# A two-layer graph network over eight graphs: one wait of VectorE moved, one row of reciprocals made on TensorE, one mean computed from a sum

## The chip, the cores and the metric

The kernel runs on one core of one Trainium2 chip. The metric is the device time of one execution in microseconds (us). The median of three runs of the kernel before is 1084.4 us, and the runs lie between 1082.91 and 1084.53 us. Engines are called TensorE (PE in the profile; PEld is its weight load), VectorE (DVE), ScalarE (ACT), GpSimd (POOL) and SyncE (SP).

## The reference, cut to what matters

There are eight graphs, each with 1024 nodes, node features `x` [1024, 256] and a dense-stored adjacency `adj` [1024, 1024] with many zeros. `W1` is [512, 256], `W2` is [256, 512] and `W` is [256, 512].

```
H   = (adj != 0);  w = adj[0, :]
D   = 1 / (H @ w)            per node,  0 where the sum is not positive
Be  = 1 / H.sum(axis=0)      per hyperedge
conv(v, W, b) = D * (H @ (Be * (H.T @ (v @ W.T)))) + b
h   = layer_norm(relu(conv(x, W1, b1)), gamma, beta)
x1  = norm(x + conv(h, W2, b2) + x)
deg = adj.sum(axis=1);  agg = (adj @ x1) / max(deg, 1e-6)
out = norm(x1 + relu(concat(x1, agg) @ W.T))
```

## The kernel before, in words

All eight graphs are worked on one core, one after the other. Nodes are cut into eight tiles of 128 and the 1024 columns into two chunks of 512. Products that need more precision than one pass gives are split into a high and a low part (`x_hi`, `x_lo` and so on).

One graph goes through these stages on TensorE, in this order. S1 forms `H.T @ x` (for graph 0 this happens in the setup, for a later graph at the end of the graph before it). S2 forms `H` times that, transposed, in four jobs: two for the first chunk of nodes (banks 2 and 3) and two for the second (banks 4 and 5). P and M, job by job (eight of each, `j`), apply `W1` to `z`, the S2 result scaled by 1/degree. Q multiplies the hidden layer `hT` by `W2` (eight jobs `i`; the first five, `Q_FIRST`, stand ahead of S3, the other three between the steps of S3). Each Q job ends with a one-column product from the sums of squares `ssum`. S3 and S4 are the second convolution, V, VM and L the second layer, and then comes S1 of the next graph. The order of the instructions on each engine is written out by hand, and semaphores join the engines.

Between S2 and P stands a chain on three engines: VectorE multiplies the S2 result by `w_row` (`scale_z`, L876), ScalarE rounds it (L609, L611), VectorE forms the low part (`take_z_low`, L882), and only then P may start. `w_row` must hold the row of 1/degree on all 128 partitions. VectorE makes 1/degree as a column, `rDn` [128, 8] (`build_rDn`, L742 to L747), and ScalarE's queue stores it to DRAM and loads it back as a row on all partitions (L602 and L599). For graphs 1 to 7 this is done in the V and L stages of the graph before. For graph 0 it is done in the setup, after VectorE's last degree sum (`sum_Dn`, L735).

In P, VectorE squares each chunk of the hidden layer (L899) and GpSimd adds the squares up (L461, semaphore `squares_summed`, six sums a graph). In Q, VectorE's `take_q(i)` (L904, L751, L911) normalises the Q job and frees its bank. Job 4 uses the bank of job 0. Two of the next graph's degree sums, for tiles 0 and 1, stand behind `take_q(5)` and `take_q(6)` (`DN_IN_Q`). They write a throwaway result into `unread_Q`, which lies on the third slot of `hpre`, the buffer that GpSimd's last sum reads. The kernel has one wait for this ahead of the first `take_q`:

```
if more:
    dve.wait_ge(squares_summed, b * NSQ + NSQ)
for i in range(NT):
    take_q(i)
    next_Dn(DN_IN_Q.get(i, ()), unread_Q)
```

`more` is false for graph 7, so that graph has no such wait.

In the setup, TensorE also forms the column mean of the scaled second weight: four f32 products of 256 columns, `mean_n` against `gW2T[:, k]`, added in one bank (L1111), in the middle of the S1 job of tile 6. ScalarE copies it out as `W2_mean` (L584) behind the first of its copies `take_m_hi` (L539), and GpSimd subtracts it from the four blocks of the weight (L426). VectorE's order there is: the split of `W1` (L824, L829), the hyperedge reciprocals (L817, L820), `take_m_lo` (L767) in turn with the last two blocks of `HT` (L774), and then the degree sums of tiles 3 to 7. After `rDn` is ready GpSimd adds `b2` to the residual in eight operations (L439).

Of the kernel before, what the change touches and what calls it, by code (L numbers as in the profile page):

```python
# [5 lines left out]
F32 = mybir.dt.float32  # L6
F32R = mybir.dt.float32r
BF16 = mybir.dt.bfloat16
ALU = mybir.AluOpType
ACT = mybir.ActivationFunctionType  # L10

P = 128
# [22 lines left out]
TRANSPOSE_BANKS = (6, 7)  # L35
N_BANKS = 8
Q_FIRST = 5
T_SLOTS = 3
FIRST_DN_AT = (4, 6)
X1_SLOTS = 3  # L40
# [2 lines left out]
DN_IN_Q = {5: (0,), 6: (1,)}  # L43
# [3 lines left out]
def graph_net(nc, x, adj, W1, b1, gamma, beta, W2, b2, WL, out):  # L47
    B, C, D = x.shape
    DH = W1.shape[0]
    NT = C // P  # L50
    ND = D // P
    NH = DH // P
    CH = 512
    NCH = C // CH
# [10 lines left out]
    NSQ = NCH * (NH - 1)  # L65
# [6 lines left out]
    N_SIDE = TRANSPOSE_BANKS[0]  # L72
# [55 lines left out]
    with ctx:  # L128
# [3 lines left out]
        def place(name, shape, dt, offset=None):  # L132
            n = 4 if dt != BF16 else 2
            for d in shape[1:]:
                n *= d
            if offset is None:
                offset = at[0]
                at[0] += (n + 63) // 64 * 64
            return nc.alloc_sbuf_tensor_at(name, shape, dt, offset=offset), offset, offset + (n + 63) // 64 * 64

        raw, raw_at, _ = place("raw", [P, NT, C], F32)
        H, H_at, _ = place("H", [P, NT, C], F32R)
# [32 lines left out]

        adjB, _, _ = place("adjB", [P, NT, NB, RB], F32, raw_at)

        yv, _, nxt = place("yv", [P, NT, YP], F32, HT_at)
        o_f32, _, nxt = place("o_f32", [P, 2, D], F32, nxt)
        unread_Q, _, _ = place("unread_Q", [P, C], BF16, hpre_at + 4 * CH * (T_SLOTS - 1))  # L180
# [17 lines left out]
        gamma_n, _, nxt = place("gamma_n", [P, P], F32, nxt)  # L198
        mean_n, _, nxt = place("mean_n", [P, P], F32, nxt)
        assert nxt <= m_lo_at + 4 * NT * D and m_lo_at == m_hi_at + 4 * NT * D  # L200
        W2_mean = ssum_0[:, 0:D]
        W1T, _, _ = place("W1T", [P, ND, DH], F32, xres_at)

        def col(n):
# [13 lines left out]
        def sem(name):  # L218
            return ctx.enter_context(nc.semaphore(name))
# [11 lines left out]
                              "gamma_loaded", "beta_loaded", "bias_loaded",  # L231
                              "table_loaded"))
        row_stored, row_loaded = sem("row_stored"), sem("row_loaded")
        rDn_dram = nc.dram_tensor("rDn_row", [C], F32)
        ident_zero, ident_ready, zero_ready, eps_ready, ones_ready, x_split, x_hi_done, xb_part, xb_ready = (
            sem(n) for n in ("ident_zero", "ident_ready", "zero_ready", "eps_ready", "ones_ready", "x_split", "x_hi_done",
# [4 lines left out]
        be_done, rBe_ready, m_hi_done = (sem(n) for n in ("be_done", "rBe_ready", "m_hi_done"))  # L241
        relu_done, squared, squares_summed, msq_done = (
            sem(n) for n in ("relu_done", "squared", "squares_summed", "msq_done"))
        mean_ready, unit_ready, W2_mean_done, W2_centred = (
            sem(n) for n in ("mean_ready", "unit_ready", "W2_mean_done", "W2_centred"))
        z_high_done, z_high_scaled, z_low_done, z_cross_done = (
            sem(n) for n in ("z_high_done", "z_high_scaled", "z_low_done", "z_cross_done"))
        W1_high_done, W1_low_done, W1_cross_done = (
# [25 lines left out]
        def emptied(stage, tile, b):  # L274

            n = bank_of[stage, tile]
            return bank_empty[n], b * fills[n] + (setup_empties[n] + nth[stage, tile] + 1)
# [10 lines left out]
        def set_empty(name, part):  # L288
            tb, turn = set_of[name, part]
            return bank_empty[tb], turn + 1  # L290
# [10 lines left out]
        def over_graphs(eng, graph):  # L301


            with eng.Fori(0, B - 1) as b:
                graph(b, True)
            graph(B - 1, False)
# [98 lines left out]
        def _(pool):  # L405
# [11 lines left out]
            def split_x(b):  # L417

                pool.wait_ge(x_hi_done, b)
                for t in range(NT):  # L420
                    nc.gpsimd.tensor_tensor(x_lo[:, t, :], x_in[:, t, :], x_hi[:, t, 0:D].bitcast(F32), ALU.subtract)\
                      .then_inc(x_split, 1)

            pool.wait_ge(W2_mean_done, 1)
            for k in range(NH):
                nc.gpsimd.tensor_tensor(gW2T[:, k, 0:D], gW2T[:, k, 0:D], W2_mean, ALU.subtract).then_inc(W2_centred, 1)  # L426
# [76 lines left out]
        def _(act):  # L503
# [75 lines left out]
                          .then_inc(W1_high_done, 1)  # L579
            for e in range(NT):  # L580
                take_m_hi("S1", e, 0, e)
                if e == 0:
                    act.wait_ge(*set_full("bW2", 0))
                    nc.scalar.activation(W2_mean, set_bank("bW2", 0)[:, D:2 * D], ACT.Copy).then_inc(W2_mean_done, 1)  # L584
                    nc.scalar.activation(bW2_row[:, :], set_bank("bW2", 0)[:, 0:D], ACT.Copy)\  # L585
                      .then_inc(bank_empty[set_of["bW2", 0][0]], 1)
# [8 lines left out]
                act.dma_start(rDn_dram.rearrange("(t p) -> p t", p=P), rDn, allow_slow_non_contiguous=True).then_inc(row_stored, 16)  # L595

            def load_rDn_row(b):
                act.wait_ge(row_stored, b * 16 + 16)
                act.dma_start(w_row[:, :], rDn_dram[:].partition_broadcast(P)).then_inc(row_loaded, 16)  # L599

            act.wait_ge(rDn_ready, 1)
            act.dma_start(rDn_dram.rearrange("(t p) -> p t", p=P), rDn, allow_slow_non_contiguous=True).then_inc(row_stored, 16)  # L602
            load_rDn_row(0)

            def graph(b, more):
                def take_z_high(ch, d):
# [110 lines left out]
        def _(dve):  # L717
# [21 lines left out]
            def build_rDn(b):  # L739

                dve.wait_ge(dn_ready, b * NT + NT)
                nc.vector.tensor_scalar(dn_pos, dn, 0.0, None, ALU.is_gt).then_inc(rDn_part, 1)  # L742
                nc.vector.tensor_scalar(dn_safe, dn, TINY, None, ALU.max).then_inc(rDn_part, 1)
                dve.wait_ge(rDn_part, b * 3 + 2)
                nc.vector.reciprocal(dn_inv, dn_safe).then_inc(rDn_part, 1)
                dve.wait_ge(rDn_part, b * 3 + 3)
                nc.vector.tensor_tensor(rDn, dn_inv, dn_pos, ALU.mult).then_inc(rDn_ready, 1)  # L747
# [117 lines left out]
            for t in range(4 + NT - N_SIDE, NT):  # L865
                sum_Dn(t, 0, unread, (first_rows_loaded[t], 16))
            build_rDn(0)

            def graph(b, more):
                dve.wait_ge(rDn_ready, b + 1)  # L870
# [58 lines left out]
                def next_Dn(tiles, into):  # L929
                    if more:  # L930
                        for c in tiles:
                            sum_Dn(c, b + 1, into, (raw_loaded[c // 2], (b + 1) * IN_B))

                if more:
                    dve.wait_ge(squares_summed, b * NSQ + NSQ)
                for i in range(NT):
                    take_q(i)
                    next_Dn(DN_IN_Q.get(i, ()), unread_Q)
                if more:
                    dve.wait_ge(q_split, b * NT + NT)  # L940
                next_Dn((2, 3), unread)
# [86 lines left out]
        def _(pe):  # L1028
# [55 lines left out]
            def transpose_set(name, part):  # L1084
                if name == "W1":
                    pe.wait_ge(W1_loaded, 16)
                    transpose_four("W1", part, [W1n[:, h, part * P:(part + 1) * P] for h in range(NH)])
                elif name == "WL":
                    pe.wait_ge(WL_loaded, 16)
                    transpose_four("WL", part, [WLn[:, o, (side * ND + part) * P:(side * ND + part + 1) * P]  # L1090
                                                for side in range(2) for o in range(ND)])
                elif name == "W2":
                    pe.wait_ge(W2_loaded, 16)
                    transpose_four("W2", part, [W2n[:, o, k * P:(k + 1) * P]
                                                for k in (2 * part, 2 * part + 1) for o in range(ND)])
                elif name == "gamma":
                    pe.wait_ge(gamma_loaded, 32)
                    tb, turn = set_of["gamma", 0]
                    pe.wait_ge(bank_empty[tb], turn)
                    nc.tensor.transpose(banks[tb][:, 0:2 * NH], gamma_n[0:2 * NH, :], ident[0:2 * NH, 0:2 * NH])\  # L1100
                      .then_inc(bank_full[tb], 1)
                else:
                    pe.wait_ge(bW2_wide_done, ND)
                    pe.wait_ge(mean_ready, 1)
                    for part in range(NH // 2):
                        pe.wait_ge(*set_empty("W2", part))
                    pe.wait_ge(W2T_scaled, NH // 2)
                    tb, turn = set_of["bW2", 0]
                    pe.wait_ge(bank_empty[tb], turn)
                    for k in range(NH):  # L1110
                        mm(banks[tb][:, D:2 * D], mean_n[:, :], gW2T[:, k, 0:D], start=(k == 0), stop=(k == NH - 1))  # L1111
                    for o in range(ND):
                        last = nc.tensor.transpose(banks[tb][:, o * P:(o + 1) * P], bW2_wide[:, o, :], ident[:, :])
                    last.then_inc(bank_full[tb], 1)
# [19 lines left out]
            for e in range(N_SIDE, NT):  # L1134
                pe.wait_ge(*free("S1", e, 0))
                for c in range(NT):
                    if e == N_SIDE and c == NT - 3:
                        transpose_set("bW2", 0)
                    s1_step(e, c, 0)
            def graph(b, more):  # L1140
                def s2_step(ch, k):

                    for d in range(ND):
                        job = ch * ND + d
                        if k == 0:
                            pe.wait_ge(*free("S2", job, b))
                        for n, m in enumerate((m_hi, m_lo)):
                            last = mm(bank("S2", job)[:, :], m[:, k, d * P:(d + 1) * P],  # L1148
                                      HT[:, k, ch * CH:(ch + 1) * CH], start=(k == 0 and n == 0),
                                      stop=(k == NT - 1 and n == 1))  # L1150
                        if k == NT - 1:
                            fills_bank(last, "S2", job)
# [8 lines left out]

                for k in range(NT):
                    s2_step(1, k)

                for j in range(NJ):
                    ch, f = j // NH, j % NH
# [86 lines left out]
                                pe.wait_ge(H_ready, (b + 1) * NT + c + 1)  # L1253
                            s1_step(e, c, b + 1)

            over_graphs(pe, graph)


# [22 lines left out]
```

## Time and profile before

| | |
|---|---|
| Median of three runs | 1084.4 us (1082.91 to 1084.53) |
| The profiled execution, its own time | 1085.47 us |
| Its span, first to last instruction | 1083.7 us |
| TensorE busy | 1045.8 us, 97% of the span |
| VectorE busy | 772.2 us, 71% |
| ScalarE busy | 432.4 us, 40% |
| GpSimd busy | 427.4 us, 39% |
| Mean granted TensorE clock | 0.990 |

The own time of the profiled execution is 1.77 us more than its span. TensorE is busy nearly all the time, so what counts is when it isn't, and at what granted clock it runs. [...] An f32 product is recorded as two instructions, so four of them are "x8".

### The profile page before, as it was taken

To read this page: it belongs to the slowest core of one execution; us is meant where nothing else is said; L and a number is where in the kernel's file an instruction comes from. 1 tells how busy PE (TensorE), PEld (TensorE's weight loads), DVE (VectorE), ACT (ScalarE), POOL (GpSimd) and SP (SyncE) were. 2 spreads that over 40 slices of the span, in tenths; PEclk is the share of its full clock that TensorE was granted. 3 is DMA by queue.
4 is the path that set the end of the run, shared out by engine and by line. 5 is a ranking of instruction groups with operands and counts; after the bars stand their busy time and mean duration, and the time that the engine had idled before them with its cause. 6 is when DMAs were issued, how large, how long until landed. Compare 5 with 4: busy or idle time off the path is not lost.

```text
span 1083.7 us, 19718 instructions
## 1 busy us (share of the span) xinstructions
PE 1045.8 (97%) x6243; PEld 939.4 (87%) x6243; DVE 772.2 (71%) x1846; ACT 432.4 (40%) x1027; POOL 427.4 (39%) x671
## 2 busy tenths in 40 slices
PE   8859999999999999999999999999999999999997
PEld 8749989798887989889898898988989889898986
DVE  6566786768857778577886687866787767867355
ACT  5353622436125362243523444243532536225350
POOL 0333535434254341553425443343535425255320
PEclk9979999999999999999999999999999999999999
DMA  7036440533407144072432634126341444400001
GB/s 286 1 98 137 98 98 20 131 82 97 106 10 174 39 99 105 17 167 74 102 76 49 146 99 100 32 69 144 97 92 24 114 99 97 97 20 1 1 2 39
DMA packets 73211, 90.44 MB, mean 83 GB/s; under 512 B 16601, under 2 KB 62305, under 8 KB 73185
## 3 DMA queue, kind: packets, MB, share of 16 engines
q1 hardware_dynamic: 63232, 85.49, 33.8%
q10 hardware_dynamic: 9952, 4.63, 1.8%
q8 instruction: 13, 0.21, 0.1%
q14 instruction: 14, 0.11, 0.0%
HBM read 81.66 MB, written 8.42 MB: 83 GB/s over the span
## 4 chain that ended last, share of the span: by engine, by line
PE 66%; issue 15%; POOL 12%; DVE 6%; ACT 1%; DMA 0%; POOLq 0%; DVEq 0%; ACTq 0%
PE bank L1047 43%; PE bank L1194 6%; POOL xres L439 4%; POOL z_cross L454 3%; POOL ssum L461 3%; PE bank L1237 3%; PE bank L1230 3%; PE bank L1231 3%; PE bank L1077 3%; DVE hpre L899 2%; PE bank L1148 1%; PE bank L1211 1%; POOL xres L433 1%; PE bank L1038 1%; ACT hpre L620 1%
## 5 line engine op out<-in xcount | busy, mean ns | idle before, releaser
L1047 PE MATMUL bank<-yv,adjT 128*128 128x257 f32 x1024 | 223.3, 379 | 0.0
L1047 PEld LDWEIGHTS bank<-yv,adjT 128*128 128x128 f32 x1024 | 193.8, 189 | 28.4
L544 ACT ACTIVATE small<-mv,small 128x1 f32<-128x1 f32 x192 | 55.9, 291 | 265.6 <-DVE mv L762 146.8
L1194 PE MATMUL bank<-gW2T,hT 128*128 128x257 f32 x512 | 125.4, 388 | 12.9 <-DVE q_f L911 12.9
L1047 PE MATMUL bank<-x_hi,H 128*128 128x256 f32 x512 | 126.4, 288 | 0.0
L1077 PE MATMUL bank<-x_hi,H 128*128 128x258 f32 x512 | 124.6, 290 | 0.0
L1047 PE MATMUL bank<-x_lo,H 128*128 128x256 f32 x512 | 123.5, 282 | 0.0
L1047 PE MATMUL bank<-m_hi,HT 128*128 128x256 f32 x512 | 122.0, 281 | 0.0
L1047 PE MATMUL bank<-m_lo,HT 128*128 128x256 f32 x512 | 121.4, 280 | 0.0
L1077 PE MATMUL bank<-x_lo,H 128*128 128x256 f32 x512 | 120.1, 283 | 0.0
L1194 PEld LDWEIGHTS bank<-gW2T,hT 128*128 128x128 f32 x512 | 93.8, 191 | 25.0 <-DVE q_f L911 13.5
L539 ACT ACTIVATE m_hi<-bank,small 128x256 fp32r<-128x256 f32 x128 | 57.5, 474 | 137.0 <-DVE small L812 76.9
L1148 PE MATMUL bank<-HT,m_lo 128*128 128x512 f32 x256 | 101.9, 398 | 0.0
L1148 PE MATMUL bank<-HT,m_hi 128*128 128x512 f32 x256 | 100.8, 394 | 0.1
L1047 PEld LDWEIGHTS bank<-x_hi,H 128*128 128x128 f32 x512 | 98.0, 191 | 0.0
L1047 PEld LDWEIGHTS bank<-x_lo,H 128*128 128x128 f32 x512 | 97.6, 191 | 0.0
L445 POOL TENSOR_TENSOR small<-mv,small 128x1 f32<-128x1 f32 x120 | 30.1, 251 | 169.6 <-DVE small L751 169.6
L767 DVE SCALAR_TENSOR_TENSOR m_lo<-bank,small,m_hi 128x256 fp32r<-128x256 f32 x128 | 59.4, 482 | 52.6 <-ACT m_hi L539 52.6
L1047 PEld LDWEIGHTS bank<-m_lo,HT 128*128 128x128 f32 x512 | 96.2, 188 | 0.0
L1047 PEld LDWEIGHTS bank<-m_hi,HT 128*128 128x128 f32 x512 | 96.1, 188 | 0.0
L1077 PEld LDWEIGHTS bank<-x_hi,H 128*128 128x128 f32 x512 | 94.2, 191 | 0.5 <-ACT bW_row L585 0.2
L1077 PEld LDWEIGHTS bank<-x_lo,H 128*128 128x128 f32 x512 | 93.5, 190 | 0.2
(125 smaller groups left out, 2191.7 us busy)
## 6 DMA issues: line engine op xcount, KB each, us to landing
raw<-in_adj_dram SPq DMA_DIRECT2D x112, 256.0 KB, 5.7
adjB<-in_adj_dram SPq DMA_DIRECT2D x224, 128.0 KB, 3.1
x_in<-in_x_dram SPq DMA_DIRECT2D x31, 256.0 KB, 6.3
out_dram<-xres SPq DMA_DIRECT2D x108, 64.0 KB, 1.6
raw<-in_adj_dram SPq DMA_DIRECT2D x8, 512.0 KB, 8.9
w_row<-in_adj_dram SPq DMA_DIRECT2D x8, 512.0 KB, 4.7
w_row<-rDn_row ACTq DMA_DIRECT2D x8, 512.0 KB, 9.2
out_dram<-xres SPq DMA_DIRECT2D x4, 256.0 KB, 2.6
```

The costliest lines, as they stand in the source:

```text
L439: nc.gpsimd.tensor_tensor(xres[:, t, :], xres[:, t, :], b2_row[:, :], ALU.add).then_inc(xb_ready, 1)
L454: nc.gpsimd.tensor_tensor(z_cross[:, d, cols], z_high[:, d, cols].bitcast(F32), z_low[:, d, cols].bitcast(F32), ALU.subtract).then_inc(z_c ...
L461: nc.gpsimd.tensor_tensor(ssum[j // NH][:, :], ssum[j // NH][:, :], hpre[:, j % T_SLOTS, :], ALU.add)\
L539: nc.scalar.activation(m_hi[:, e, :], bank(stage, e)[:, 0:D], ACT.Identity, scale=rBe[:, e:e + 1])\
L544: nc.scalar.activation(std[:, i:i + 1], mv[:, which, i, 1:2], ACT.Sqrt, bias=eps_c)\
L767: empties_bank(nc.vector.scalar_tensor_tensor(out=m_lo[:, e, :], in0=bank(stage, e)[:, 0:D], scalar=rBe[:, e:e + 1], in1=m_hi[:, e, :].bit ...
L1047: last = mm(bank(stage, i)[:, 0:n_cols], lhsT, rhs, start=(k == 0 and part == 0), stop=(k == NT - 1 and part == parts - 1))
L1077: last = mm(*args, start=(c == 0 and n == 0), stop=(c == NT - 1 and n == 1))
L1148: last = mm(bank("S2", job)[:, :], m[:, k, d * P:(d + 1) * P], HT[:, k, ch * CH:(ch + 1) * CH], start=(k == 0 and n == 0), stop=(k == NT - ...
L1194: mm(bank("Q", i)[:, 0:D + 1], hT[:, k, i * P:(i + 1) * P], gW2T[:, k, :], start=(k == 0), stop=(k == NH - 1))
L1230: mm(bank("V", i)[:, :], x1_high[n][:, part], WL_high[:, d, :], start=(d == 0), stop=False)
L1231: last = mm(bank("V", i)[:, :], x1_low[:, n, part], WL_low[:, d, :], start=False, stop=(d == ND - 1))
```

## The change

VectorE's wait for `squares_summed` goes from ahead of the first `take_q` to just ahead of each of the two degree sums in `DN_IN_Q`. For graph 0, VectorE fills a 128x128 tile of ones and multiplies the identity by `rDn`, both broadcast, into eight diagonal blocks; TensorE multiplies the ones by the diagonals, two f32 products of 512 columns into banks 0 and 1, behind the third step of S2's second chunk; ScalarE copies the two banks to `w_row`. The store and the load through DRAM remain for graphs 1 to 7. For this TensorE's program has graph 0 written out ahead of its loop, which then runs over graphs 1 to 6. For the mean, GpSimd adds the four blocks of the weight in three dependent operations, TensorE makes one product of the sum, and ScalarE takes the result behind its sixth copy `take_m_hi` and not behind the first.

```diff
+        diagonals, _, nxt = place("diagonals", [P, NT, P], F32, raw_at)
+        ones, _, _ = place("ones", [P, P], F32, nxt)
...
+            pool.wait_ge(W2T_scaled, NH // 2)
+            for part in range(NH // 2):
+                pool.wait_ge(*set_empty("W2", part))
+            for k in range(1, NH):
+                if k > 1:
+                    pool.wait_ge(W2_summed, k - 1)
+                nc.gpsimd.tensor_tensor(W2_sum, gW2T[:, 0, 0:D] if k == 1 else W2_sum, gW2T[:, k, 0:D], ALU.add)\
+                  .then_inc(W2_summed, 1)
             pool.wait_ge(W2_mean_done, 1)
...
                 take_m_hi("S1", e, 0, e)
-                if e == 0:
+                if e == N_SIDE - 1:
                     act.wait_ge(*set_full("bW2", 0))
...
-                act.wait_ge(row_stored, b * 16 + 16)
+                act.wait_ge(row_stored, b * 16)
...
-            act.wait_ge(rDn_ready, 1)
-            act.dma_start(rDn_dram.rearrange("(t p) -> p t", p=P), rDn, allow_slow_non_contiguous=True).then_inc(row_stored, 16)
-            load_rDn_row(0)
+            for ch in range(NCH):
+                act.wait_ge(row_full, ch + 1)
+                nc.scalar.activation(w_row[:, ch * CH:(ch + 1) * CH], banks[ROW_BANKS[ch]][:, :], ACT.Copy)\
+                  .then_inc(row_loaded, 16 // NCH)
...
             build_rDn(0)
+            nc.vector.memset(ones[:, :], 1.0).then_inc(ones_set, 1)
+            dve.wait_ge(rDn_ready, 1)
+            dve.wait_ge(ident_ready, 1)
+            nc.vector.tensor_tensor(diagonals[:, :, :], ident[:, :].unsqueeze(1).to_broadcast([P, NT, P]),
+                                    rDn.unsqueeze(2).to_broadcast([P, NT, P]), ALU.mult).then_inc(diagonals_done, 1)
...
-                if more:
-                    dve.wait_ge(squares_summed, b * NSQ + NSQ)
                 for i in range(NT):
                     take_q(i)
-                    next_Dn(DN_IN_Q.get(i, ()), unread_Q)
+                    if more and i in DN_IN_Q:
+                        dve.wait_ge(squares_summed, b * NSQ + NSQ)
+                        next_Dn(DN_IN_Q[i], unread_Q)
...
-                    for part in range(NH // 2):
-                        pe.wait_ge(*set_empty("W2", part))
-                    pe.wait_ge(W2T_scaled, NH // 2)
+                    pe.wait_ge(W2_summed, NH - 1)
                     tb, turn = set_of["bW2", 0]
                     pe.wait_ge(bank_empty[tb], turn)
-                    for k in range(NH):
-                        mm(banks[tb][:, D:2 * D], mean_n[:, :], gW2T[:, k, 0:D], start=(k == 0), stop=(k == NH - 1))
+                    mm(banks[tb][:, D:2 * D], mean_n[:, :], W2_sum, start=True, stop=True)
...
+            def make_row():
+                pe.wait_ge(ones_set, 1)
+                pe.wait_ge(diagonals_done, 1)
+                for ch in range(NCH):
+                    pe.wait_ge(*emptied("S1", ROW_BANKS[ch], 0))
+                    mm(banks[ROW_BANKS[ch]][:, :], ones[:, :], diagonals[:, ch * 4:ch * 4 + 4, :],
+                       start=True, stop=True).then_inc(row_full, 1)
...
                 for k in range(NT):
                     s2_step(1, k)
+                    if first and k == ROW_BEHIND:
+                        make_row()
...
-            over_graphs(pe, graph)
+            graph(0, True, True)
+            with pe.Fori(1, B - 1) as b:
+                graph(b, True)
+            graph(B - 1, False)
```

## Rows read from the trace of the kernel before

**Rows 1.** The page's busy time of each engine, with share and instructions.

```profile
PE 1045.8 (97%) x6243; PEld 939.4 (87%) x6243; DVE 772.2 (71%) x1846; ACT 432.4 (40%) x1027; POOL 427.4 (39%) x671
```

**Rows 2.** TensorE's waits: who for whom, us in total, times, longest.

```profile
PE bank L1174 <- DVE z_low L882: 13.9, 1, 13.9
PE bank L1194 <- DVE q_f L911: 12.9, 7, 2.0
```

**Rows 3.** Timeline of graph 1's Q: start, us, instruction, idle and releaser.

```profile
206.73 1.91 PE L1194 MATMUL bank<-gW2T,hT 128*128 128x257 f32 x8
...
215.33 0.22 DVE L904 SCALAR_TENSOR_TENSOR mv<-bank,mv 128x1 f32<-128x1 f32 x1 [2.50 <-POOL ssum L461]
...
216.64 2.01 PE L1194 MATMUL bank<-gW2T,hT 128*128 128x257 f32 x8 [2.00 <-DVE q_f L911]
```

**Rows 4.** The same timeline for graph 7, which lacks the wait.

```profile
990.96 1.91 PE L1194 MATMUL bank<-gW2T,hT 128*128 128x257 f32 x8
...
996.94 0.21 DVE L904 SCALAR_TENSOR_TENSOR mv<-bank,mv 128x1 f32<-128x1 f32 x1
...
998.73 1.99 PE L1194 MATMUL bank<-gW2T,hT 128*128 128x257 f32 x8
...
999.52 1.33 POOL L465 TENSOR_TENSOR x_lo<-q_f,x_hi 128x256 fp32r<-128x256 f32 x2
```

**Rows 5.** Windows of graph 2 behind its wait; PEclk stands behind POOL.

```profile
346.80:350.00 3.20, 3.19 (x12) 2.77 (x13) 1.63 (x7) 1.81 (x9) 1.39 (x3) 0.69 1.02 210
350.00:353.30 3.30, 3.30 (x19) 3.08 (x18) 1.42 (x5) 0.75 (x4) 1.36 (x2) 0.78 0.74 153
```

**Rows 6.** Timeline: the row's way in graph 0, and graph 1's first P job.

```profile
44.97 0.40 ACTq L602 DMA_DIRECT2D rDn_row<-small  x1
45.07 5.57 POOL L439 TENSOR_TENSOR xres<-xres,b_row 128x256 f32<-128x256 f32 x8 [8.58 <-DVE small L747]
...
60.51 1.29 DVE L876 TENSOR_TENSOR z_f<-bank,w_row 128x512 f32<-128x512 f32 x2 [15.57 <-DMA w_row<-rDn_row]
...
65.05 0.80 PE L1174 MATMUL bank<-z_high,W_high 128*128 128x512 f32 x1 [13.93 <-DVE z_low L882]
65.07 1.29 POOL L454 TENSOR_TENSOR z_cross<-z_high,z_low 128x512 fp32r<-128x512 f32 x1 [0.62 <-DVE z_low L882]
...
195.53 0.39 PE L1174 MATMUL bank<-z_high,W_high 128*128 128x512 f32 x1
```

**Rows 7.** TensorE's timeline: the first and the last of graph 0's 64 S2 products.

```profile
35.94 0.47 PE L1148 MATMUL bank<-HT,m_hi 128*128 128x512 f32 x1
...
50.71 0.40 PE L1148 MATMUL bank<-HT,m_lo 128*128 128x512 f32 x1
```

**Rows 8.** TensorE's timeline of graph 0: Q's job 0 and job 4.

```profile
77.73 1.90 PE L1194 MATMUL bank<-gW2T,hT 128*128 128x257 f32 x8
...
86.48 2.01 PE L1194 MATMUL bank<-gW2T,hT 128*128 128x257 f32 x8 [0.84 <-DVE q_f L911]
```

**Rows 9.** Timeline of the setup: the mean, its copy, its user, VectorE behind it.

```profile
30.81 1.89 PE L1111 MATMUL bank<-gW2T,mean_n 128*128 128x256 f32 x8
...
32.96 0.38 ACT L584 ACTIVATE ssum<-bank 128x256 f32<-128x256 f32 x1 [2.02 <-PE bank L1113]
...
33.42 3.07 POOL L426 TENSOR_TENSOR gW2T<-gW2T,ssum 128x256 f32<-128x256 f32 x4 [31.83 <-ACT ssum L584]
...
34.01 0.48 DVE L767 SCALAR_TENSOR_TENSOR m_lo<-bank,small,m_hi 128x256 fp32r<-128x256 f32 x1 [1.95 <-ACT m_hi L539]
```

**Rows 10.** Timeline: one VectorE operation beside GpSimd's work and without it.

```profile
140.61 5.35 POOL L421 TENSOR_TENSOR x_lo<-x_in,x_hi 128x256 fp32r<-128x256 f32 x8 [3.99 <-DVE H L724]
...
142.17 0.72 DVE L1008 SCALAR_TENSOR_TENSOR xres<-o_f,xres 128x256 f32<-128x256 f32 x1
...
149.11 0.42 DVE L1008 SCALAR_TENSOR_TENSOR xres<-o_f,xres 128x256 f32<-128x256 f32 x1
```

**Rows 11.** VectorE's operations of 1024 elements with two SBUF inputs: count, busy, mean ns.

```profile
L735 DVE SCALAR_TENSOR_TENSOR unread<-raw,w_row 128x1024 bf16<-128x1024 f32 x50 | 61.0, 1220 | 9.5 <-POOL x_lo L465 9.1
```

More of the change, by code:

```diff
@@ L37 @@
 Q_FIRST = 5
+ROW_BANKS = (0, 1)
+ROW_BEHIND = 2
 T_SLOTS = 3
@@ L200, in graph_net @@
         assert nxt <= m_lo_at + 4 * NT * D and m_lo_at == m_hi_at + 4 * NT * D
-        W2_mean = ssum_0[:, 0:D]
+        W2_mean, W2_sum = ssum_0[:, 0:D], ssum_0[:, D:2 * D]
         W1T, _, _ = place("W1T", [P, ND, DH], F32, xres_at)
@@ L233, in graph_net @@
         row_stored, row_loaded = sem("row_stored"), sem("row_loaded")
+        ones_set, diagonals_done, row_full = sem("ones_set"), sem("diagonals_done"), sem("row_full")
         rDn_dram = nc.dram_tensor("rDn_row", [C], F32)
@@ L243, in graph_net @@
             sem(n) for n in ("relu_done", "squared", "squares_summed", "msq_done"))
-        mean_ready, unit_ready, W2_mean_done, W2_centred = (
-            sem(n) for n in ("mean_ready", "unit_ready", "W2_mean_done", "W2_centred"))
+        mean_ready, unit_ready, W2_summed, W2_mean_done, W2_centred = (
+            sem(n) for n in ("mean_ready", "unit_ready", "W2_summed", "W2_mean_done", "W2_centred"))
         z_high_done, z_high_scaled, z_low_done, z_cross_done = (
@@ L1139, in _, with graph @@
                     s1_step(e, c, 0)
-            def graph(b, more):
+            def make_row():
[5 more added lines that the diff above has]
+                       start=True, stop=True).then_inc(row_full, 1)
+            def graph(b, more, first=False):
                 def s2_step(ch, k):
```

## The prediction

> **What bounds the kernel now.** I read the busy times first: TensorE is busy for 97% of the span, so no other engine's share can matter except where TensorE waits for it [rows 1]. Next I read TensorE's own waits. Two entries hold 26.8 us: once 13.9 us before the first P product, and seven times, 12.9 us in all and 2.0 us at most, in Q [rows 2]. The change works on just these two places. Then I followed each in the timeline.
>
> In Q of graph 1, VectorE stands idle for 2.50 us until GpSimd's last sum is there, starts `take_q(0)` at 215.33, and TensorE, which needs the bank of job 0 for job 4, starts again at 216.64 after 2.00 us [rows 3]. Graph 7 has no such wait in its program: there `take_q(0)` has no idle time before it and job 4 follows at once [rows 4]. It is a built-in view of the kernel without the wait. [...]
>
> In graph 0, VectorE has `rDn` ready by 45.07 (GpSimd's release), but the row is on all partitions only at 60.51, after 15.57 us of idle time on VectorE, and P starts at 65.05 [rows 6]. TensorE's last S2 product began at 50.71 [rows 7].
>
> **The wait in Q.** Nothing is removed but order: the same sums and the same degree sums are done. From the start of job 0 to that of job 4 graph 1 takes 216.64 - 206.73 = 9.91 us [rows 3] and graph 7 takes 998.73 - 990.96 = 7.77 us [rows 4]. The difference is 2.14 us. Graphs 1 to 6 all wait 2.00 us, graph 0 waits 0.84 us and takes 86.48 - 77.73 = 8.75 us, 0.98 over graph 7 [rows 8]. That is 6 x 2.14 + 0.98 = 13.8 us. The fallen clock costs 3.20 x 0.31 + 3.30 x 0.22 = 1.7 us in graph 2 [rows 5] and as much in graph 6, 3.4 us together. I count it as gained, since it begins where TensorE's idle time ends. Sum: 17.2 us.
>
> What is late next? VectorE is free at 215.33 - 2.50 = 212.83, and `take_q(0)` frees the bank 216.64 - 215.33 = 1.31 us after it starts, so at 214.14, 7.41 us after job 0 began [rows 3]. TensorE gets to job 4 at 7.77 us. There is 0.36 us to spare, little, but on the right side. The one-column product of job 4 waits for the same sums, yet only behind job 4's four products, and S3 needs GpSimd's first `x_lo`, which in graph 7 starts 8.56 us after job 0 without any idle time on TensorE [rows 4]. The wait now stands ahead of the degree sums of tiles 0 and 1; behind it are `take_q(6)`, `take_q(7)` and VectorE's S3 work. It costs nothing, because `take_q(5)` needs Q's job 5, which is filled after job 4 and so after all sums. SP's loads are tied to the ends of P and Q, so they move with TensorE. Bounds: 13.8 us if the two falls of the clock come back elsewhere, 17.2 us if not.
>
> **The mean.** Four products of 256 columns take 1.89 us; one takes a quarter, so TensorE's S2 starts 1.4 us earlier, near 34.5 instead of 35.94 [rows 7, 9]. GpSimd's three dependent additions cost it some 2.4 us (3.07 / 4 = 0.77 each for independent ones [rows 9]). GpSimd is idle for 31.83 us before its first use [rows 9], and the second half of the weight is copied well before 30.81, so TensorE should not wait. ScalarE no longer stands in front of the bank of the mean with four `m_hi` copies behind it, so VectorE's 1.95 us of idle time at 34.01 goes [rows 9]. On the other side, GpSimd's additions run beside the splitting of `W1` and its subtractions (3.07 us) move beside the degree sum of tile 3. A VectorE operation with two SBUF inputs took 0.72 us beside GpSimd and 0.42 us alone, 1.7 times as long [rows 10]. I put back 1.15 us for this. Then `rDn` is ready 0.8 us earlier, at 44.3. Bounds: 43.1 (the whole 1.95 gained) and 45.07 (nothing).
>
> **The row.** It has these steps. (a) The fill with ones is an operation of 128 columns, about 0.1 us. (b) The diagonals have 1024 elements and two SBUF inputs. The nearest row is the degree sum, 1.22 us [rows 11]. But GpSimd's eight additions, 5.57 us, are released by the same `rDn` [rows 6], so I take 1.22 x 1.7 = 2.1 us. With one semaphore the diagonals are there at 44.3 + 2.3 = 46.6. Bounds: 1.22 and 2 x 1.22 us, so 44.5 to 47.7. (c) TensorE passes the third step of the second chunk, 44 of 64 products at (50.71 - 35.94) / 63 = 0.234 us each [rows 7], at 34.5 + 10.3 = 44.8. It waits for 1.8 us, until R = 46.6; R lies between 44.8 and 47.7. (d) Two f32 products of 512 columns have the columns of the four of 256, 1.89 us [rows 9]; this is new work on TensorE. (e) ScalarE's copy of 256 columns takes 0.38 us [rows 9], one of 512 perhaps 0.6. The row stands at R + 1.9 + 0.1 + 0.6 = R + 2.6. (f) From there to P it took 65.05 - 60.51 = 4.54 us [rows 6], so P starts at R + 7.1. TensorE has the row and the remaining 20 products behind it at R + 1.9 + 4.7 = R + 6.6, and waits another 0.5 us. (g) P's first M job needs GpSimd's second `z_cross`, which started with P and took 1.29 us [rows 6], while four P products at 0.234 take 0.94: 0.4 us more. In effect P starts at R + 7.5 = 54.1.
>
> Before, P started at 65.05, and P and its neighbour to Q took 77.73 - 65.05 = 12.68 us [rows 6, 8] against 206.73 - 195.53 = 11.20 in graph 1 [rows 3, 6]; 1.48 us went to the clock that had fallen in the long wait. So the old effective start is 66.5 and the gain 66.5 - 54.1 = 12.4 us. Bounds: R = 44.8 gives 14.2, R = 47.7 gives 11.3.
>
> [...]
>
> **TensorE's loop.** Graph 0 is now a copy of its own. Graph 7 is also run from a copy of its own, and its P stage to Q is entered as in graph 1: its job 0 to 4 of Q show no gap [rows 4]. I cost this at nothing; above it I have no row.
>
> **The sum.** 17.2 + 12.4 = 29.6 us off the profiled execution's 1085.47: 1055.9 us. That execution is 1.07 us above the median of 1084.4, less than one fall of the clock costs (1.7 us). I read this as one fall more in it than in a middling run, and since the new kernel should have none, I start from the profiled one. From the median the same step would be 28.5 us.
>
> **The rivals.**
>
> 1. *The clock falls in other places.* Graph 0 keeps short waits of 1.8, 0.5 and 0.4 us. Waits of 2.0 us brought the clock down in two cases of six. One fall costs 1.7 us, two cost 3.4: 1057.6 to 1059.3. For it: the first of these waits is nearly as long. Against it: five waits in Q did nothing. Chance 0.15.
>
> 2. *GpSimd blocks the diagonals wholly.* They then run behind the eight additions: 44.3 + 5.6 + 1.3 = 51.2 = R. P starts in effect at 58.7, a gain of 7.8 us, less 1.7 us for a clock that falls in a wait of 6.4 us. The total is 23.3 us: 1062.2. Against it stands 1.7 times, not more, beside eight additions in a row [rows 10]. Chance 0.08.
>
> 3. *The wait in Q is replaced.* The spare time is only 0.36 us, and VectorE's steps now run beside GpSimd's last sums. If TensorE still waits for 1 us in each of seven graphs, Q gives 10.2 us and the total is 22.6: 1062.9. If it is the whole 2.0 us (the change doesn't do what it says), 12.4 us remain: 1073.1. Against both stands graph 7. Chance 0.07.
>
> 4. *Slower.* Entering the loop at graph 1 for the first time could make TensorE wait for code that it had met before in graph 0. It decides if this one place costs over 29.6 us; with 35 us the time is 1090.9. Nothing in the trace shows such a gap at the entry of graph 7's copy. Chance 0.02.
>
> **How the numbers follow.** The forecast has the remaining 0.68; its own range is 1054.1 (R = 44.8) to 1057.0 (R = 47.7), and half a microsecond either way for differences of executions. With the first rival this holds 0.83, and the range is 1053.6 to 1059.6. The bound of what a measurement can tell is 0.2%, 2.2 us. All cases but the fourth are faster by more: 0.97. Same: 0.01. Slower: 0.02.
>
> **What would show it.** Right: no TensorE wait for `q_f` in graphs 0 to 6, 7.8 us from job 0 to job 4, and a clock of 1.00 behind it; the diagonals done near 46.6 in over 2 us beside GpSimd; P's first product near 53.7; the mean's product under 0.5 us. Wrong: a wait of job 4 or S3 in its place; the diagonals taking over 4 us; an S2 that waits for the last `m_lo`, which VectorE now must have ready 1.4 us sooner; low granted clock in graph 0 behind the row.

## The result and the profile after

The changed kernel takes 1055.93 us (median of four runs, 1055.58 to 1056.11), the kernel before 1083.87 us (median of four runs, one more than was known before; 1082.91 to 1084.53). The ratio is 0.9742 with a 95% interval of 0.9726 to 0.9759: 27.9 us, 2.6% faster. The profiled execution of the changed kernel also takes 1055.93 us and has a span of 1054.1 us. The forecast was 1055.9 us, so the total was met; but that it was met so closely is luck: inside it, two steps were wrong and cancelled each other.

The page of the changed kernel, busy time of each engine, against [rows 1]:

```profile
PE 1040.4 (99%) x6241; PEld 934.0 (89%) x6241; DVE 774.5 (73%) x1848; ACT 433.5 (41%) x1029; POOL 430.1 (41%) x674
```

TensorE's waits in the changed kernel, against [rows 2]:

```profile
PE bank L1059 <- DMA raw<-in_adj_dram: 4.5, 1, 4.5
PE bank L1098 <- ACT bW_row L600: 1.6, 1, 1.6
PE bank L1202 <- DVE z_low L903: 1.0, 1, 1.0
PE bank L1059 <- ACT adjT L564: 0.6, 1, 0.6
PE bank L1210 <- POOL z_cross L469: 0.2, 1, 0.2
```

The 13.9 us ahead of P have become 1.0 and the 12.9 us in Q are gone from the list. A new row stands there: TensorE waits 1.6 us for ScalarE's copy of the mean's bank (L600). The forecast had no such row.

Graph 1's Q in the changed kernel, timeline of all engines, against [rows 3]:

```profile
193.42 1.90 PE L1222 MATMUL bank<-gW2T,hT 128*128 128x257 f32 x8
...
199.08 2.91 POOL L476 TENSOR_TENSOR ssum<-ssum,hpre 128x512 f32<-128x512 f32 x2 [0.71 <-DVE hpre L920]
...
199.44 0.21 DVE L925 SCALAR_TENSOR_TENSOR mv<-bank,mv 128x1 f32<-128x1 f32 x1
...
200.21 0.48 DVE L932 SCALAR_TENSOR_TENSOR q_f<-bank,small,bW_row 128x256 f32<-128x256 f32 x1
...
201.19 1.99 PE L1222 MATMUL bank<-gW2T,hT 128*128 128x257 f32 x8
...
201.94 1.34 POOL L480 TENSOR_TENSOR x_lo<-q_f,x_hi 128x256 fp32r<-128x256 f32 x2
```

VectorE now starts `take_q(0)` at 199.44, beside GpSimd's last sums, and is through with it at 200.69. TensorE starts job 4 at 201.19, 7.77 us after job 0, exactly as graph 7 did before [rows 4]. The bank is free 0.5 us before it is needed. The granted clock in this place, a share of full speed, in windows of graphs 1, 2 and 6 (PEclk behind POOL), against [rows 5]:

```profile
193.00:201.00 8.00, 8.00 (x41) 7.00 (x40) 6.95 (x12) 4.83 (x11) 4.39 (x4) 1.00 0.77 177
321.00:329.00 8.00, 8.00 (x41) 6.99 (x40) 6.98 (x12) 4.79 (x11) 4.38 (x5) 1.00 0.82 187
833.00:841.00 8.00, 8.00 (x41) 6.99 (x40) 7.00 (x12) 4.77 (x11) 4.38 (x5) 1.00 0.82 179
```

From Q to Q every graph now takes 128.0 us. Before, it was 129.0 us from graph 0 to 1, 130.2 us behind each later graph, and 131.8 us where the clock fell. From Q's job 0 of graph 0 to that of graph 7 it is 896.1 us; before, it was 913.2. These 17.1 us are what the moved wait gave between the two profiled executions.

The setup of graph 0, timeline, against [rows 6, 9]:

```profile
30.70 0.59 PE L1129 MATMUL bank<-ssum,mean_n 128*128 128x256 f32 x2
...
32.41 0.48 DVE L783 SCALAR_TENSOR_TENSOR m_lo<-bank,small,m_hi 128x256 fp32r<-128x256 f32 x1
...
33.32 0.43 ACT L600 ACTIVATE bW_row<-bank 128x256 f32<-128x256 f32 x1
...
33.55 4.71 POOL L441 TENSOR_TENSOR gW2T<-gW2T,ssum 128x256 f32<-128x256 f32 x4 [4.26 <-ACT ssum L599]
...
33.80 0.39 PE L1098 MATMUL bank<-x_hi,H 128*128 128x258 f32 x1 [1.58 <-ACT bW_row L600]
...
35.81 0.40 PE L1174 MATMUL bank<-HT,m_hi 128*128 128x512 f32 x1
...
43.23 1.20 DVE L887 TENSOR_TENSOR diagonals<-ident,small 128x1024 f32<-128x1024 f32 x1
...
43.31 6.55 POOL L454 TENSOR_TENSOR xres<-xres,b_row 128x256 f32<-128x256 f32 x8 [5.05 <-DVE small L763]
...
46.08 1.88 PE L1163 MATMUL bank<-diagonals,ones 128*128 128x512 f32 x4
...
48.39 0.60 ACT L618 ACTIVATE w_row<-bank 128x512 f32<-128x512 f32 x1 [0.59 <-PE bank L1163]
...
49.02 1.29 DVE L897 TENSOR_TENSOR z_f<-bank,w_row 128x512 f32<-128x512 f32 x2 [4.59 <-ACT w_row L618]
...
51.98 1.55 DVE L903 SCALAR_TENSOR_TENSOR z_low<-z_f,z_cross 128x512 fp32r<-128x512 f32 x1 [0.35 <-ACT z_cross L627]
...
53.67 0.47 PE L1202 MATMUL bank<-z_high,W_high 128*128 128x512 f32 x1 [1.04 <-DVE z_low L903]
...
65.38 1.90 PE L1222 MATMUL bank<-gW2T,hT 128*128 128x257 f32 x8
```

The mean is one product, recorded as two instructions (x2), of 0.59 us, but S2 starts at 35.81, hardly before the old 35.94 [rows 7]. The diagonals take 1.20 us and are done at 44.43, and TensorE comes to the row's products 1.65 us later, at 46.08, without waiting for anything. P starts at 53.67 in place of 65.05 [rows 6], and Q's job 0 at 65.38 in place of 77.73 [rows 8].

### The profile page after: what moved, and what is told of

The parts are those of the page before. It is cut to its first block, busy times and chain, and to the rows that moved or that the text cites. A ratio compares the mean times of both kernels' runs of the same rounds, so it can differ in the third digit from the quotient of the medians.

```text
span 1054.1 us, 19674 instructions
## 1 busy us (share of the span) xinstructions
PE 1040.4 (99%) x6241; PEld 934.0 (89%) x6241; DVE 774.5 (73%) x1848; ACT 433.5 (41%) x1029; POOL 430.1 (41%) x674
## 4 chain that ended last, share of the span: by engine, by line
PE 96%; DVE 1%; POOL 1%; issue 1%; DMA 0%; ACT 0%; POOLq 0%; DVEq 0%; ACTq 0%
PE bank L1068 44%; PE bank L1098 11%; PE bank L1222 11%; PE bank L1174 10%; PE bank L1210 3%; PE bank L1258 3%; PE bank L1265 3%; PE bank L1203 3%; PE bank L1259 3%; PE bank L1202 3%; PE bank L1239 1%; PE bank L1059 1%; PE bank L1225 1%; DVE unread L751 1%; POOL xres L454 0%
## 5 line engine op out<-in xcount | busy, mean ns | idle before, releaser
L1222 PEld LDWEIGHTS bank<-gW2T,hT 128*128 128x128 f32 x512 | 93.0, 190 | 11.5
## 6 DMA issues: line engine op xcount, KB each, us to landing
adjB<-in_adj_dram SPq DMA_DIRECT2D x224, 128.0 KB, 3.3
```

The source lines that it names most:

```text
L1222: mm(bank("Q", i)[:, 0:D + 1], hT[:, k, i * P:(i + 1) * P], gW2T[:, k, :], start=(k == 0), stop=(k == NH - 1))
```

## The experiments

The kernel before was run again beside each group; its median was 1083.01 us beside the first four, 1083.93 beside the next four and 1084.09 beside the last two.

**The moved wait alone, on the kernel before.**

```diff
-                if more:
-                    dve.wait_ge(squares_summed, b * NSQ + NSQ)
                 for i in range(NT):
                     take_q(i)
-                    next_Dn(DN_IN_Q.get(i, ()), unread_Q)
+                    if more and i in DN_IN_Q:
+                        dve.wait_ge(squares_summed, b * NSQ + NSQ)
+                        next_Dn(DN_IN_Q[i], unread_Q)
```

> The kernel before with the moved wait alone. Theory (graph 7 shows what is left): TensorE has no wait for q_f in any graph, 7.8 us from job 0 to job 4 of Q in graphs 1 to 6; 13.8 us less, and up to 3.4 us more where the clock fell in the run compared: 1067 to 1070 us. Rival (only the idle time counts and the clock falls anyway): 12.9 us less and the granted clock still falls below 0.85 in Q of some graph: 1071 us or more.

Measured: 1067.35 us, ratio 0.9861 (0.9845 to 0.9877), 15.7 us less. TensorE has no wait for `q_f` left. From Q to Q the graphs take 128.0 us each, and no fall of the clock is left in Q; from job 0 of graph 0 to that of graph 7 it is 896.1 us, as in the changed kernel. If 13.8 us of the 15.7 are stall, 1.9 us remain, more than one fall of the clock and less than two. The rival falls: the clock did not fall elsewhere.

**The row alone, on the kernel before.** The edit is the row's part of the diff above, with the old wait and the old mean.

> The kernel before with the row of graph 0 made on TensorE alone. rDn stays at 45.1; the diagonals are done at 46.4; the row's products start at 46.4 and P near 54.1. Theory: P's gain is 12.0 us, but graph 0 then waits 2.0 us in Q as the other graphs do and not 0.84, since P no longer runs at a low clock: net 10.8 us less, about 1073 us. Rival (the two parts add up without touching each other): 12 us less and still 0.8 us of wait in graph 0's Q, 1072 us; the profile's wait decides.

Measured: 1071.51 us, ratio 0.9901 (0.9885 to 0.9918), 11.5 us less. TensorE's waits in this kernel:

```profile
PE bank L1217 <- DVE q_f L924: 13.0, 7, 2.0
...
PE bank L1205 <- POOL z_cross L461: 1.2, 1, 1.2
```

Q's job 0 starts at 65.47, 12.26 us sooner than before and within 0.1 us of the whole change's 65.38. That already says what the mean is worth in company. The row's products start at 45.94 and P at 52.75, sooner than the 46.4 and 54.1 that were expected: the single diagonals operation took 1.20 us here too and ended at 45.84. Graph 0's wait in Q is 0.95 us, so neither 2.0 (theory) nor 0.84 unchanged (rival): the first M job waited 1.2 us here, and the engines that sum the squares lag TensorE less for it. That this is the cause is argued, not tested; the expected net gain of 10.8 us was 0.7 too small.

**The mean alone, on the kernel before.**

> The kernel before with the second weight's mean alone. Theory: TensorE saves 1.3 us on the products and loses 1.6 us in front of S1's tile 7, whose bank ScalarE now empties late, so S2 starts at 35.8 to 35.9 as before; but VectorE has rDn 1.8 us sooner (43.3), and since the row's way through DRAM decides P, the time falls by about 1.8 us, to 1082 us. Rival 1 (the products' time counts): S2 starts near 34.5. Rival 2 (no path is touched): no change, P at 65.0.

Measured: 1081.61 us (1080.46 to 1084.96), ratio 0.9994 (0.9985 to 1.0004). The time can't be told from no change. The median is 1.4 us below the 1083.01 of the kernel before beside it, but two of the ten runs took 1084.9 us, at a mean granted clock of 0.988 against 0.991 or 0.992 in the others. The profile can be read in spite of it. Timeline of its setup:

```profile
33.23 0.39 PE L1092 MATMUL bank<-x_hi,H 128*128 128x258 f32 x1 [1.58 <-ACT bW_row L600]
...
42.44 0.17 DVE L762 TENSOR_TENSOR small<-small 128x8 f32<-128x8 f32 x1
...
42.64 0.40 ACTq L617 DMA_DIRECT2D rDn_row<-small  x1
...
53.25 0.36 ACTq L614 DMA_DIRECT2D w_row<-rDn_row  x1
...
57.17 1.29 DVE L891 TENSOR_TENSOR z_f<-bank,w_row 128x512 f32<-128x512 f32 x2 [14.57 <-DMA w_row<-rDn_row]
```

TensorE loses 1.58 us at S1's tile 7, for a bank that ScalarE empties late, and gains 1.3 us on the products: nothing. VectorE has `rDn` sooner: it starts the last operation for it at 42.44, against 44.63 in the kernel with the wait alone, whose setup is the old one. S2 starts at 35.24 here and at 35.80 there, and of these 0.6 us some are inputs that landed sooner in this run, so `rDn` gained about 1.7 us. P starts at 61.72. The row's way through DRAM, though, took 57.17 - 42.64 = 14.5 us here, 60.51 - 44.97 = 15.5 us in the profile before [rows 6] and 59.08 - 44.83 = 14.3 us in the kernel with the wait alone, whose way is the old one; it varies by about as much as the effect. The theory's path is seen, its 1.8 us is not shown in the time.

**The old wait, put back in the changed kernel.**

> The changed kernel with the old wait in Q put back. Theory: seven waits of 2.0 us, graph 0 included, each 2.14 us from job 0 to job 4, so 15.0 us more than the changed kernel, and 0 to 3.4 us for falls of the clock behind them: 1071 to 1074.5 us, with a wider spread than 0.6 us between runs. Rival (graph 0 keeps its 0.84): 13.8 us more.

Measured: 1071.76 us (1071.67 to 1072.18), 15.8 us more than the changed kernel. Graph 0 waits 1.52 us, six graphs 2.0 us each, and the clock fell once. The changed kernel was not run beside this one: the kernel before had a median of 1083.01 us here and 1083.87 there, so some 0.9 us of this difference are open. The two profiles need no such comparison: from Q's job 0 of graph 0 to that of graph 7 it is 912.2 us against 896.1, 16.1 us more. The theory's sum holds; its 2.0 us for graph 0 was too much, the rival's 0.84 too little. The spread of 0.5 us between runs is no wider than that of the changed kernel; a wider one had been expected.

**ScalarE's copy of the mean behind the second `m_hi`, not the sixth.**

```diff
-                if e == N_SIDE - 1:
+                if e == 1:
                     act.wait_ge(*set_full("bW2", 0))
```

> The changed kernel with ScalarE's copy of the mean behind its second m_hi copy instead of the sixth. Theory (the late copy made TensorE wait 1.58 us at S1's tile 7 and ate the 1.3 us that the single product saves): the wait falls to 0.2 us, S2 starts at 34.4 instead of 35.8, VectorE keeps its early rDn (43.2), the row's products start at 44.8 instead of 46.08, and the time falls by 1.3 us to 1054.6. Rival (the row waits for the diagonals or GpSimd, not for TensorE): the products still start near 46 and the time stays at 1055.9.

Measured: 1054.67 us (1054.17 to 1054.89), 1.3 us less than the changed kernel's 1055.93. TensorE's wait for the copy is gone (0.2 us had been expected), S2 starts at 34.52 and the products of the row at 44.88. The theory of the wait holds, and the rival falls. But P's first M job now waits longer, and in the profiled executions Q's job 0 comes only 1.0 us sooner (64.42 against 65.38). TensorE's waits and GpSimd's timeline in this kernel:

```profile
PE bank L1210 <- POOL z_cross L469: 1.2, 1, 1.2
...
PE bank L1202 <- DVE z_low L903: 0.2, 1, 0.2
```

```profile
50.87 3.07 POOL L469 TENSOR_TENSOR z_cross<-z_high,z_low 128x512 fp32r<-128x512 f32 x2 [0.63 <-DVE z_low L903]
```

GpSimd's two `z_cross` operations now stand back to back behind its additions, and the first of P's M jobs waits for the second. P itself starts 6.8 us behind the row's products and not 7.6: VectorE's second `z_low` takes 1.55 us in the changed kernel, beside GpSimd's first `z_cross`, while here, with GpSimd still at its additions, the two `z_low` together take 1.74 us. That GpSimd's operation is the cause is argued, not tested.

**The row's products one step sooner.**

```diff
-ROW_BEHIND = 2
+ROW_BEHIND = 1
```

> The changed kernel with the row's products behind the second step of S2's second chunk instead of the third. The diagonals are done at 44.4 and the second step ends at 45.15, so theory: products at 45.15, no wait for the diagonals, P 0.9 us sooner, 1055.0 us. The wait of the first M job for GpSimd's z_cross may grow from 0.2 to 1 us, since GpSimd's eight additions end at 49.9 whatever happens; if that rival decides, the time stays within 0.3 us of 1055.9.

Measured: 1054.60 us (1054.34 to 1054.81), 1.3 us less than the changed kernel. The products stand right behind the second step, 9.34 us behind S2's start against 10.27 us in the changed kernel, which is the 0.9 us expected; the M job's wait stays at 0.2 us, so the rival falls. In the profiled run another 0.4 us come from S2, which started at 35.42 and not at 35.81. The edit doesn't touch that part; unchanged setups started S2 between 35.65 and 35.80 us in three other profiles, so this is taken as a difference between executions. How much of it is in the medians is open.

**Both.**

> Both edits. S2 starts at 34.4, its second step of the second chunk ends at 43.8, the diagonals are done at 44.5: TensorE waits about 0.7 us for them, products at 44.6. Theory: 0.2 us better than the copy alone, 1054.4 us. Rival (GpSimd's additions, which end near 49.9, hold the first z_cross): same as the better of the two single edits, 1054.6 to 1055.0.

Measured: 1054.31 us (1054.20 to 1054.68), ratio 0.9717 (0.9699 to 0.9736) to the kernel before. TensorE waits 0.9 us for the diagonals, which end at 44.30, 0.1 us ahead of the product at 44.40 (the profile itself names no releaser for this wait), and 0.7 us for `z_cross`. The two edits together give 1.6 us and not 1.3 + 1.3: the diagonals and GpSimd have come close to the path. This is the lowest median of the study, but it is only 0.3 and 0.4 us below those of the single edits, no more than the spread within each, so the order of the three is not shown.

**The row's products behind all of S2.**

```diff
-ROW_BEHIND = 2
+ROW_BEHIND = 7
```

> The changed kernel with the row's products behind the last step of S2, so with no work of TensorE behind them. Products at 50.8, P at 50.8 + 7.6 = 58.4, TensorE waits 5.7 us there instead of 1.04. Theory: 4.7 us more for the later row, and 1 to 1.6 us for a granted clock that falls in the wait: 1060.6 to 1062.2 us. Rival (the remaining S2 steps cover nothing, since the chain through VectorE, ScalarE and GpSimd sets P): no more than 1 us slower.

Measured: 1061.49 us (1061.20 to 1062.20), 5.6 us more than the changed kernel. TensorE waits 5.7 us ahead of P. Windows of this wait and of P's start:

```profile
52.00:58.00 6.00, 0.62 (x2) 0.00 (x0) 3.36 (x4) 3.23 (x6) 1.26 (x1) 0.98 0.00 1
58.00:62.00 4.00, 3.69 (x10) 2.99 (x11) 2.72 (x5) 2.75 (x5) 2.53 (x2) 0.60 0.41 97
```

This is the price of the cover: the five S2 steps behind the row hide most of the chain through ScalarE and VectorE, and when they don't, the granted clock of P's first 4 us is 0.60: windows of 1 us from 58 to 62 give 0.50, 0.50, 0.50 and 0.91. Q's job 0 comes 5.5 us later, at 70.89: 4.7 us are the longer wait, and the other 0.9 us lie between P's start and Q, behind the fall of the clock. The theory holds, and the rival falls.

**GpSimd's additions sooner, on the kernel with both edits.**

```diff
             pool.wait_ge(bias_loaded, 16)
-            pool.wait_ge(rDn_ready, 1)
```

> The kernel with both edits, and GpSimd's eight additions to the residual no longer wait for rDn; they start when ScalarE has written the residual, near 40.7. Theory (in the kernel with both edits the first M job waits 0.72 us for z_cross because the additions end at 49.8): they end before 48, the first z_cross starts right behind the first z_low, the wait falls to 0.2 us, and 0.5 us go: 1053.8 us. Rival: the additions slow down VectorE's last degree sums, rDn and the row come later by up to 1 us, and nothing is gained: 1054.3 us or more.

Measured: 1056.54 us (1055.60 to 1056.78), 2.2 us more than without the edit. VectorE's timeline in this kernel, with GpSimd's:

```profile
40.85 1.56 DVE L750 SCALAR_TENSOR_TENSOR unread<-raw,w_row 128x1024 bf16<-128x1024 f32 x1
...
42.45 0.58 DVE L757 TENSOR_SCALAR small<-small 128x8 f32<-128x8 f32 x1
...
43.78 1.68 DVE L886 TENSOR_TENSOR diagonals<-ident,small 128x1024 f32<-128x1024 f32 x1
```

```profile
40.58 7.51 POOL L453 TENSOR_TENSOR xres<-xres,b_row 128x256 f32<-128x256 f32 x8 [5.70 <-ACT xres L603]
```

Now GpSimd is there first. VectorE's last degree sum takes 1.56 us instead of 1.22, an operation of eight columns 0.58 instead of 0.17, the diagonals 1.68 instead of 1.20. TensorE waits 2.27 us, until 45.56, 0.1 us after the diagonals end, and the clock falls behind this wait. Windows before and behind it:

```profile
41.00:45.50 4.50, 2.29 (x10) 1.50 (x8) 4.35 (x8) 0.00 (x0) 4.50 (x5) 1.00 0.00 0
45.50:49.00 3.50, 3.44 (x6) 1.60 (x7) 0.00 (x0) 0.60 (x1) 2.59 (x4) 0.60 0.00 0
```

The rival is right. The wait for `z_cross` (0.7 us) is gone, as the theory said, but it was worth less than the 1.4 us by which the wait for the diagonals grew and the fall of the clock behind it.

**The diagonals in four operations, in the changed kernel.**

```diff
-            nc.vector.tensor_tensor(diagonals[:, :, :], ident[:, :].unsqueeze(1).to_broadcast([P, NT, P]),
-                                    rDn.unsqueeze(2).to_broadcast([P, NT, P]), ALU.mult).then_inc(diagonals_done, 1)
+            for q in range(4):
+                part = nc.vector.tensor_tensor(diagonals[:, 2 * q:2 * q + 2, :],
+                                               ident[:, :].unsqueeze(1).to_broadcast([P, 2, P]),
+                                               rDn[:, 2 * q:2 * q + 2].unsqueeze(2).to_broadcast([P, 2, P]), ALU.mult)
+                part.then_inc(diagonals_done, 1)
```

> The changed kernel with the diagonals made by four VectorE operations of 256 elements instead of one of 1024. [...] The time hardly moves, since TensorE comes to the row 1.6 us after the diagonals are done. [...]

Measured: 1056.07 us in a single run, within the changed kernel's range of 1055.58 to 1056.11. VectorE's and GpSimd's rows in its timeline:

```profile
43.18 3.04 DVE L888 TENSOR_TENSOR diagonals<-ident,small 128x256 f32<-128x256 f32 x4
...
43.26 6.31 POOL L454 TENSOR_TENSOR xres<-xres,b_row 128x256 f32<-128x256 f32 x8 [5.04 <-DVE small L763]
```

The same 1024 elements take 3.04 us in four pieces and 1.20 us in one, both times beside GpSimd's eight additions and with VectorE first by 0.08 us; the additions took 6.31 us beside the four and 6.55 beside the one. Part of the 1.8 us is the price of the cutting itself, which was not measured without GpSimd; four VectorE operations of 256 elements that read a bank and one SBUF input take 1.66 us in the changed kernel (`take_m_lo`), which by estimate makes that part about 0.5 us.

## Why the prediction was right, point by point

**The wait in Q: right.** The term was 17.2 us, 13.8 of them stalls and 3.4 falls of the clock. These are the falls of graphs 2 and 6 in the profile before: windows of 1 us give 0.50, 0.50, 0.50 and 0.79 from 348 to 352 us, and 0.62, 0.50, 0.50 and 0.67 from 870 to 874, 1.7 us lost in each; behind the waits of the other five graphs the clock is 1.00. Graph 0's Q starts at 65.38 and the span ends at 1054.1, that is 988.7 us; before, it was 1083.7 - 77.73 = 1006.0. The difference is 17.2 us, and 17.1 of them lie between the Q of graph 0 and that of graph 7. The slack was given as 0.36 us, from 7.41 to 7.77; the trace after has 0.5. Both experiments on it agree, one taking the wait away from the old kernel (15.7 us) and one putting it back in the new (15.8 us). They lie below 17.2, since the clock fell twice in the profile before and once in each of the profiles of three other kernels with the wait: of 24 waits of 2.0 us in four profiles, five were followed by a fall, at some 1.6 us each. The reading that the profiled execution held about one fall more than a middling run fits these. It isn't the only one: in that execution the row's way through DRAM also took 15.5 us, and 14.3 and 14.5 us in the two other profiles that have it, so up to 1.2 us of its excess can be this.

**The mean: a step that failed.** The prediction said that S2 starts 1.4 us earlier, near 34.5. It starts at 35.81. The step missed that the bank of the mean is also the bank of S1's tile 7, so the later copy, which it counted only as a gain for VectorE, holds TensorE for 1.58 us. Moving the copy to the second place took the wait away and brought S2 to 34.52: this is shown. The median fell by 1.3 us, the profiled execution by 1.0. On VectorE's side it expected the full 1.95 us less 1.15 us for GpSimd's work beside it, a figure for which it gave no working. The trace has `rDn` at 43.31 and not 44.3: of the 1.95 us only 0.2 were lost. The splitting of `W1` was indeed stretched, its first two operations from 1.29 to 1.86 us together and the next two from 1.29 to 1.83, but only 0.45 us of this 1.1 us reached the next operation (at 30.36, before at 29.91), since VectorE had been idle there. The second `HT` operation, now ahead of GpSimd's subtractions, took 0.69 us and not 0.99. The degree sums beside GpSimd's subtractions took 1.22 and 1.38 us, and it was GpSimd that grew, from 3.07 [rows 9] to 4.71 us.

**The row: right in its sum, with two errors in it.** R was put at 46.6, set by the diagonals, with a wait of 1.8 us. It was 46.08, set by TensorE, with no wait. The diagonals were mis-sized: 1.20 us, not 2.1. The two errors cancelled: TensorE 1.3 us later than thought, the diagonals 2.2 us sooner than thought (44.43 against 46.6, of which 1.0 us is the earlier `rDn` and 0.9 us the operation). Had the mean done what was said and the diagonals taken 1.20 us, R would have been 44.8 and the forecast 1.8 us too high. The kernel with the copy in second place is nearly that case: R is 44.88 and the time 1054.67 us. So it is luck that the total was met to 0.1 us. The rest held: the two products with the 20 S2 products behind them took 52.63 - 46.08 = 6.55 us (6.6 were said), the row was there at R + 2.9 (2.6) because the copy of the second bank started 1.19 us behind the first, P came at R + 7.6 (7.1), the M job waited 0.2 us more (0.4). The fill with ones, put at 0.1 us without a row, took 0.17 us, and the diagonals began 0.08 us behind its start. In effect P starts 12.35 us sooner, counted at Q's job 0 (12.4 were said).

**VectorE's operations beside GpSimd's: half right.** That GpSimd's work can stretch them is seen again: the first two operations of the splitting of `W1` took 1.86 us, beside its additions of the weight's blocks, and 1.29 us before. The factor of 1.7 was carried from a short operation of 256 elements [rows 10] to one of 1024, and that was the mistake: the short one had lost 0.30 us, and the diagonals took 1.20 us when they began 0.08 us ahead of GpSimd's additions and 1.68 us when these were already running, never 2.1. The second rival, a full block, falls as well: the diagonals ended at 44.43, GpSimd's additions at 49.86. Three rows fit the reading that it matters which engine has begun: the diagonals' 1.20 us, their 1.68, and the degree sum that began beside the running additions and took 1.56 us and not 1.22. Another does not: a degree sum that began at 34.97, beside GpSimd's subtractions that had run since 33.55, kept its 1.22 us. The four short operations took 1.8 us more than the one long, some 0.5 of it perhaps by the cutting. What decides between these cases was not shown.

**The first and the third rival: did not come.** Behind the waits of 1.6, 1.0 and 0.2 us in the changed kernel the clock stayed at 1.00. It fell behind waits of 5.7, 2.27 and sometimes 2.0 us, and not behind 1.2 us in two experiments. No wait stands at job 4 of Q in place of the old one, so the third rival falls too.

**TensorE's loop: right.** The fourth rival did not come. With graph 0 written out, no gap shows at the entry of graph 1; the time from Q to Q is 128.04 us between graphs 0 and 1 and 128.03 between 1 and 2.

**Against the median:** 28.5 us were said from there and 27.9 measured.

## What to carry to other kernels

If one pass of a loop lacks the wait that a change removes, its rows give the new pace, and the slack behind it, better than any sum of durations. When a copy out of a bank is moved later, look up who fills that bank next, not only who stands behind the copy on its own engine. And do not trust a sum that comes out right: here a part worth about 1.3 us was lost in one place and hidden by a price that was set too high in another, and only the single waits of the trace told so.

## What the runs showed of the hardware

GpSimd's eight additions took 5.57 us alone and 6.55 us with the diagonals beside them. A VectorE operation of eight columns took 0.58 us and not 0.17 when it began beside GpSimd's running additions; the next one, beside the same additions, took 0.16 us. Cutting one VectorE operation of 1024 elements into four made it 2.5 times as long, 3.04 against 1.20 us, beside GpSimd; the four were not run without GpSimd.

Behind TensorE's waits of 1.6 us and less its clock did not fall in any profile here; behind those of 2.0 us it fell in five cases of 24, and during or behind those of 2.27, 5.7 and 11.4 to 13.9 us each time (five cases). The lowest window of 1 us in each of these ten falls has a clock of 0.50. The wait of 4.5 us for the first input, ahead of TensorE's first product, is not counted.
